# A chain of eight transformer layers on one core: three bias additions taken from TensorE to GpSimd and VectorE

## The reference

```python
x = x + _L0_attn_ref(_layernorm(x), ...)   # delta rule
x = x + _L0_ffn_ref(_layernorm(x), ...)    # the sine layer
x = x + _L1_attn_ref(_layernorm(x), ...)   # test-time MLP
x = x + _L1_ffn_ref(_layernorm(x), ...)    # dense experts
x = x + _L2_attn_ref(_layernorm(x), ...)   # softmax attention
x = x + _L2_ffn_ref(_layernorm(x), ...)    # channel mix
x = x + _L3_attn_ref(_layernorm(x), ...)   # blocked attention
x = x + _L3_ffn_ref(_layernorm(x), ...)    # routed experts
```

```python
# sine layer
hidden = jnp.einsum('bsd,df->bsf', x, W1) + b1
q = _quantum_transform(hidden, quantum_phases, quantum_weights_real, quantum_weights_imag)
return jnp.einsum('bsf,fd->bsd', jax.nn.relu(q), W2) + b2
# dense experts
gate_logits = jax.nn.softmax(x @ gate_w + gate_b, axis=-1)
# blocked attention, after the heads
return out @ out_w.T + out_b
```

## Time and profile before

| | us |
|---|---|
| median of 3 runs | 2658.85 |
| lowest, highest | 2652.12, 2659.35 |
| the profiled execution: its own time | 2652.55 |
| its span | 2650.7 |

### The profile page before, as it was taken

One profiled execution on the slowest core, in us unless ns is written; L12 is line 12 of the kernel. 1 busy time (PEld: TensorE's weight loads), 2 busy tenths in 40 slices (PEclk: granted clock), 3 DMA queues, 4 the chain that ended last, 5 costly groups with the idle time before them and its releaser, 6 DMA issues.

```text
span 2650.7 us, 63819 instructions
## 1 busy us (share of the span) xinstructions
PE 2092.7 (79%) x19997; PEld 1174.4 (44%) x20060; DVE 1837.0 (69%) x3796; ACT 1329.5 (50%) x2738; POOL 489.6 (18%) x920
## 2 busy tenths in 40 slices
PE   4449876788888778549999975569999999999755
PEld 2336543467777553224444434323333333333434
DVE  4856647556555447758888864579999999998371
ACT  4311105443333220327777763548888888888312
POOL 4312330034444210101111110001111111111103
PEclk9755558799999869869999997769999999999677
DMA  2342210000000000031111100221111111111001
GB/s 60 79 111 67 70 47 9 7 0 0 0 0 0 1 8 0 28 96 32 34 33 32 35 16 0 65 67 37 36 36 36 36 36 36 36 36 28 19 0 32
DMA packets 140453, 86.47 MB, mean 33 GB/s; under 512 B 67166, under 2 KB 119783, under 8 KB 140330
## 3 DMA queue, kind: packets, MB, share of 16 engines
q1 hardware_dynamic: 140330, 84.81, 12.8%
HBM read 56.88 MB, written 27.26 MB: 32 GB/s over the span
## 4 chain that ended last, share of the span: by engine, by line
PE 49%; DVE 28%; issue 10%; ACT 6%; DMA 2%; SPq 2%; POOL 2%; DVEq 1%; POOLq 0%; ACTq 0%; another core or an unknown queue 0%; PEldq 0%
PE psum L2098 9%; PE psum L2120 9%; DVE ba_blockmax L2330 8%; PE psum L2109 6%; DVE X L1285 2%; PE psum L2129 2%; PE psum L649 2%; PE psum L409 1%; ACT tt_sg L1638 1%; DVE dn_arena L929 1%; DVE tt_aT L1693 1%; PE psum L638 1%; PE psum L1600 1%; PE psum L672 1%; PE psum L1609 1%
## 5 line engine op out<-in xcount | busy, mean ns | idle before, releaser
L2330 DVE TENSOR_REDUCE ba_blockmax<-psum 128x16 f32<-128x1024 f32 x512 | 606.9, 1214 | 57.6 <-PE psum L2098 37.4
L2202 ACT ACTIVATE ba_pt<-psum 128x512 f32<-128x512 f32 x1024 | 554.0, 597 | 102.5 <-PE psum L2109 86.0
L2098 PE MATMUL psum<-ba_ks,ba_qs 64*128 64x512 bf16 x1024 | 343.7, 416 | 63.4 <-DMA ba_ks<-ba_kstk 21.2
L2332 DVE TENSOR_REDUCE sa_negmax<-psum 128x1 f32<-128x1024 f32 x256 | 304.4, 1221 | 85.8 <-PE psum L2098 77.9
L2202 ACT ACTIVATE sa_pt<-psum 128x512 f32<-128x512 f32 x512 | 269.9, 599 | 116.3 <-remote 58.7
L2120 PE MATMUL psum<-ba_pt,ba_vh 128*32 128x256 f32 x4096 | 314.1, 390 | 0.3
L2109 PE MATMUL psum<-ba_qs,ba_ks 64*128 64x512 bf16 x1024 | 313.7, 380 | 0.8 <-ACT ba_pt L2202 0.4
L2098 PE MATMUL psum<-sa_ks,sa_qs 96*128 96x512 bf16 x512 | 207.4, 410 | 30.8 <-DMA sa_ks<-sa_kstk 23.9
L2098 PEld LDWEIGHTS psum<-ba_ks,ba_qs 64*128 64x128 bf16 x1024 | 117.0, 148 | 253.8 <-issue 251.2
L2109 PE MATMUL psum<-sa_qs,sa_ks 128*128 128x512 bf16 x449 | 170.7, 383 | 1.8 <-ACT sa_pt L2202 1.6
L2120 PEld LDWEIGHTS psum<-ba_pt,ba_vh 128*32 128x32 f32 x4096 | 92.3, 108 | 154.8 <-issue 146.8
(11 more groups left out here) (479 smaller groups left out, 3902.6 us busy)
## 6 DMA issues: line engine op xcount, KB each, us to landing
ba_qs<-ba_qstk SPq DMA_DIRECT2D x128, 48.0 KB
ba_ks<-ba_kstk SPq DMA_DIRECT2D x128, 48.0 KB
dn_pst<-dn_arena SPq DMA_DIRECT2D x32, 128.0 KB, 2.4
dn_tst<-dn_arena SPq DMA_DIRECT2D x8, 512.0 KB, 5.8
dn_arena<-dn_tst SPq DMA_DIRECT2D x8, 512.0 KB, 4.4
dn_arena<-dn_pst SPq DMA_DIRECT2D x8, 512.0 KB, 5.9
ba_qs<-ba_qstk SPq DMA_DIRECT2D x128, 32.0 KB
ba_ks<-ba_kstk SPq DMA_DIRECT2D x128, 32.0 KB
```

What stands on the lines that cost most here:

```text
L2098: last = nc.tensor.matmul(bank(2 * slot + h), qs[b][0:KP, :].rearrange("p (a r) -> p r a", r=NTB)[:, r, :], ks[b][0:KP, h * HALF:(h + 1) * ...
L2202: nc.scalar.activation(pt[x_][:, :, h * P:(h + 1) * P].rearrange("p j (a m) -> p j a m", m=2), bank(4 + slot).rearrange("p (a j m) -> p j ...
L2330: ins = nc.vector.tensor_reduce(blockmax[g][:, r, :], src.rearrange("p (n s) -> p n s", s=BLOCK), AXX, ALU.max, negate=True)
L2332: ins = nc.vector.tensor_reduce(negmax[g][:, r:r + 1], src, AXX, ALU.max, negate=True)
```

## The change

The three one-row products are gone, and the first product of each group clears the bank in their place (start=True at n_ == 0 and f == 0, at n == 0, at m == 0). The biases are laid out as 128 equal rows, and are added

- in the sine layer and in the projection by GpSimd, directly to `k.X`, in eight instructions of 128x512 for each layer, issued back to back once the normalised tiles are all in `k.XT` and the weights are in. VectorE's own addition to the same tiles waits for a new semaphore `biased`, raised by one for each group;
- in the experts' gate by VectorE, whose copy out of PSUM becomes an addition.

```diff
@@ sine_ffn
-    b2 = k.sb("sf_b2", [1, GT], ctx=ctx)
+    b2 = k.sb("sf_b2", [P, D], ctx=ctx)
+    biased = k.sem("sf_biased")
 def add(i, g):
             v.wait_ge(outp[g], i + 2)
+            v.wait_ge(biased, i * 2 + g + 1)
+            k.plain(v)
-            nc.tensor.matmul(k.psum[:, 4 + g, :], k.ones_row[:, :], b2[:, :], start=True, stop=True)
             for n_ in range(GROUP):
                 for f in range(NF):
                     last = nc.tensor.matmul(k.psum[:, 4 + g, n_ * D:(n_ + 1) * D], act[g][:, f, n_ * P:(n_ + 1) * P],
-                                            w2[:, f, :], start=False, stop=True, skip_group_check=True)
+                                            w2[:, f, :], start=n_ == 0 and f == 0, stop=True, skip_group_check=True)
+    def gpsimd(p):
+        p.wait_ge(w_in, 64)
+        for g in range(2):
+            p.wait_ge(xt[g], NG // 2 + 1)
+        for n in range(NG):
+            xs = k.X[:, n * GROUP:(n + 1) * GROUP, :]
+            nc.gpsimd.tensor_tensor(xs, xs, b2[:, :].unsqueeze(1).to_broadcast([P, GROUP, D]), ALU.add).then_inc(biased, 1)
@@ dense_experts
-    gb = k.sb("de_gb", [1, GROUP * E], ctx=ctx)
+    gb = k.sb("de_gb", [P, E], ctx=ctx)
-                nc.tensor.matmul(bank, k.ones_row[:, :], gb[:, :], start=True, stop=True)
-                                            start=False, stop=True, skip_group_check=True)
+                                            start=n == 0, stop=True, skip_group_check=True)
-                nc.vector.tensor_copy(lg[:, bass.ds(i * 2 * GROUP + g * GROUP, GROUP), :],
-                                      k.psum[:, g, 0:GROUP * E].rearrange("p (n e) -> p n e", e=E)).then_inc(taken[g], 1)
+                nc.vector.tensor_tensor(lg[:, bass.ds(i * 2 * GROUP + g * GROUP, GROUP), :],
+                                        k.psum[:, g, 0:GROUP * E].rearrange("p (n e) -> p n e", e=E),
+                                        gb[:, :].unsqueeze(1).to_broadcast([P, GROUP, E]), ALU.add).then_inc(taken[g], 1)
@@ project_out
-                nc.tensor.matmul(k.psum[:, 2 + g, :], k.ones_row[:, :], ob[:, :], start=True, stop=True)
-                                            start=False, stop=True, skip_group_check=True)
+                                            start=m == 0, stop=True, skip_group_check=True)
                 v.wait_ge(outp[g], b + 1)
+                v.wait_ge(biased, 2 * b + g + 1)
+    def gpsimd(p):
+        p.wait_ge(w_in, 32)
+        for g in range(2):
+            p.wait_ge(xt[g], NG // 2 + 1)
+        for n in range(NG):
+            xs = k.X[:, n * GROUP:(n + 1) * GROUP, :]
+            nc.gpsimd.tensor_tensor(xs, xs, ob[:, :].unsqueeze(1).to_broadcast([P, GROUP, D]), ALU.add).then_inc(biased, 1)
```

More of the change, by code:

```diff
@@ L409, in second_product @@
                     last = nc.tensor.matmul(k.psum[:, 4 + g, n_ * D:(n_ + 1) * D], act[g][:, f, n_ * P:(n_ + 1) * P],
-                                            w2[:, f, :], start=False, stop=True, skip_group_check=True)
+                                            w2[:, f, :], start=n_ == 0 and f == 0, stop=True, skip_group_check=True)
             last.then_inc(outp[g], 1)
         one_ahead(t, NG, first_product, second_product)
-    k.add(sync=sync, vector=vector, scalar=scalar, tensor=tensor)
+    def gpsimd(p):
[5 more added lines that the diff above has]
+            nc.gpsimd.tensor_tensor(xs, xs, b2[:, :].unsqueeze(1).to_broadcast([P, GROUP, D]), ALU.add).then_inc(biased, 1)
+    k.add(sync=sync, vector=vector, scalar=scalar, tensor=tensor, gpsimd=gpsimd)
 def delta_net(k):
@@ L1244, in vector @@
         c = Chain(v, own)
+        v.wait_ge(w_in, 64)
         with v.Fori(0, NG // 2) as i:
@@ L2396, in attention, with project_out @@
     if blocked:
-        project_out(k, tag, O, H, HD, all_done, 1)
-def project_out(k, tag, O, H, HD, head_done, N):
+        project_out(k, tag, O, H, HD, all_done, 1, xt)
+def project_out(k, tag, O, H, HD, head_done, N, xt):
     nc, d, ctx = k.nc, k.dram, k.layer_ctx
@@ L2404, in project_out @@
     ow = k.sb(f"{tag}_ow", [P, D], ctx=ctx)
-    ob = k.sb(f"{tag}_ob", [1, GT], ctx=ctx)
+    ob = k.sb(f"{tag}_ob", [P, D], ctx=ctx)
+    biased = k.sem(f"{tag}_biased")
     oT = [k.sb(f"{tag}_ooT{z}", [P, S], ctx=ctx) for z in range(2)]
@@ L2859, in lay_out @@
                                                   col("L0_ffn_quantum_weights_real"), col("L0_ffn_quantum_weights_imag")], 1))
-    a["sf_b2"] = np.tile(a["L0_ffn_b2"], GROUP)[None]
+    a["sf_b2"] = np.tile(a["L0_ffn_b2"], (P, 1))
     a["dn_wqkv"] = np.concatenate([a[f"L0_attn_W{n}"] for n in "qkvb"], 1)
@@ L2871, in lay_out @@
     a["cm_mu"] = np.ascontiguousarray(np.stack([a["L2_ffn_mu_r"], a["L2_ffn_mu_k"]], 1))
-    a["de_gb"] = np.tile(a["L1_ffn_gate_b"], GROUP)[None]
+    a["de_gb"] = np.tile(a["L1_ffn_gate_b"], (P, 1))
     a["de_ew"] = np.ascontiguousarray(a["L1_ffn_expert_w"].transpose(1, 0, 2).reshape(D, -1))
@@ L2885, in lay_out @@
     a["ba_ow"] = np.ascontiguousarray(a["L3_attn_out_w"].T)
-    a["ba_ob"] = np.tile(a["L3_attn_out_b"], GROUP)[None]
+    a["ba_ob"] = np.tile(a["L3_attn_out_b"], (P, 1))
     for tag, heads in (("sa", 8), ("ba", 16)):
```

## The result

| | us |
|---|---|
| changed kernel, median of 4 runs | 2620.35 (2614.38 to 2622.89) |
| kernel before, median of 4 runs | 2659.1 (2652.12 to 2664.32) |
| ratio | 0.9853, interval 0.9824 to 0.9882 |
| span of the profiled executions, before and after | 2650.7, 2616.7 |

The account below looks back on a forecast made before the run. The prediction took TensorE's chain of waits, with the one-row products on it, as the bound in the three stretches. Its terms, −28.27 + 8.5 + 0.15 = −19.6 us, counted from 2655.7, gave 2636 us; range 2621 to 2651.

Parts of the forecast that it names:

- The products stand on the path, and go whole.: Sine layer, gate, projection: one-row products lie on TensorE's chain; removing them saves 11.55 + 4.47 + 12.25 = 28.27 us.
- Nothing late takes their place.: Sine layer, gate, projection: VectorE and ScalarE work uncovers no new wait; additions on VectorE's own path cost together 0.15 us.
- The GpSimd train holds the small columns, 8.5 us.: Sine layer's start: eight GpSimd additions hold eight of nine small VectorE steps, L309 to L320, delaying the first L366 8.5 us.
- The train before the projection ends just in time.: Before the projection: eight GpSimd additions end at 2463.0, ahead of L2352 at 2463.63; cover 0.6 us, cost put at 0.
- the heads' other work stays clear of it: Before the projection: the rest of VectorE's work for earlier heads reads PSUM or is early; no cost given.
- So the whole 28.3 us should go, if the clock keeps its pattern.: Sine layer, gate, projection: the full 28.3 us of removed products is gained, provided TensorE's clock pattern stays.
- Rival D: Sine layer stays at half clock, more idle and less work between waits: +26 to +35 us, 2667, slower; chance 0.06.
- Rival C: Sine layer and projection: gain partly lost to TensorE's clock, with a late train; together +8.7 us, 2645; chance 0.20.
- B: Sine layer's start: VectorE gets in between GpSimd's additions, 1.2 us lost in place of 8.5; −26.9, 2629; chance 0.20.
- The chance of 0.80 for faster: Whole kernel: chance 0.80 of being faster by over 0.3%, against 0.14 within 0.3% and 0.06 slower.

Follow-up runs that it names:

- e1: Changed kernel with an unused one-row product put back where the sine layer's and projection's bias products stood: 2662.03 us, ratio 1.0022 against the kernel before.
- e2: Changed kernel with an unused 128-row product put back where the sine layer's and projection's bias products stood: 2634.37 us, ratio 0.9915 against the kernel before.
- e7: Kernel before with its sine-layer and projection bias products kept but made 128 rows wide: 2632.77 us against 2662.58, ratio 0.9892.
- e8: Kernel before with only the projection's part of the change: 2636.06 us, ratio 0.9901 against the kernel before.

## Why the prediction was right and wrong

- **The products stand on the path, and go whole.** Right. L411 starts behind L378, and put back they cost their 1.1 us and more (e1, e2).
- **Nothing late takes their place.** Right: no new wait is seen in the chains of the three stages; ScalarE's copies hold 1.1 us of the projection's chain after as before, now 7.4% of it.
- **The GpSimd train holds the small columns, 8.5 us.** Right in mechanism, one VectorE step for each addition, tensor_scalar of four columns included. The size was 7.4 (27.4 - 19.9 us to the first L369) and 6.1 in the second profile (26.1 - 19.9): the additions follow each other 1.23 us apart, not 1.34, and the train began a step or two later in the columns. The 1.34 was from two additions of which the second needs the first. The Trainium skill's rule ("SBUF — State Buffer", Who interferes with whom) is borne out by these rows, also for tensor_scalar on four columns, which the forecast had left open.
- **The train before the projection ends just in time.** It did, and with more room than forecast: from 2436.17 it takes 9.90 us, to 2446.07, and the last head's step came at 2447.85. The cover was 1.8 us. But the forecast that the heads' other work stays clear of it was wrong: one step of the head before met the train and took 1.01 us, where its like took 0.22 in the kernel before. It isn't on the chain.

```profile
2442.67 1.01 DVE L2376 TENSOR_TENSOR XT<-ba_oS,ba_recip 128x64 f32<-128x64 f32 x1
```
- **"So the whole 28.3 us should go, if the clock keeps its pattern."** This is the step that failed: the sum gives the clock a term of 0, and no row is shown for that. The clock did not keep its pattern. Sine layer: -9.8 measured is -11.55 for the products, +7.4 for the train, +0.1, and -5.7 left over; the blocks of 32 passes alone went from 38.0 us (35.8% of 106) to 30.6 (eight of 3.83), and other pieces of the layer took 1.7 of these 7.4 back. Projection: -20.0 is -12.25 and -7.7. Gate and experts: -7.1 is -4.5 and -2.6. Together 16.0 us of the miss; e7 finds about 20 of clock in the first two when the products are kept. The other 3.2 of the 19.2 us are a train 1.1 us cheaper than forecast, less 2.9 that the untouched layers gave back, and 4.8 by which the medians lie further apart than the profiled executions; for the last two the record has no cause.
- **The gate's -2.6 can't be put down to the change.** Its loop, before and after, and two stretches of it after:

```profile
959.00:978.00 19.00, 18.91 (x80) 18.13 (x80) 1.34 (x7) 5.47 (x8) 0.00 (x0) 0.50 0.00 0
```
```profile
948.00:952.00 4.00, 2.81 (x24) 2.46 (x22) 0.38 (x2) 2.94 (x7) 0.00 (x0) 1.00 0.00 0
...
956.00:960.00 4.00, 4.00 (x20) 4.00 (x21) 0.57 (x3) 2.52 (x3) 0.00 (x0) 0.50 0.00 0
```

  Before, the loop ran at half clock from its start; after, it starts at full clock and falls to half, with no one-row product in it. But in e7 and e8, whose gate is that of the kernel before, it also starts at full clock and takes 16.9 and 17.2 us in place of 18.9, and in e2, whose gate is the changed one, it runs at 0.51 and takes 13.7 in place of 11.6.
- **Rival D** had the direction backwards. It reasoned that with the products gone each group has less work for the clock to see. The rows to doubt that stood there: TensorE was busy for 33.41 of 35 us in the projection, and its clock 0.60. An engine that is busy all the time at a low clock says that its busy time alone doesn't tell its clock. I read these two numbers side by side and drew only the price from them.
- **Rival C** priced the clock in the same wrong direction, and counted two turns in the projection where the chain has four (17.4% of 35 us is 6.1); **B** (a cheap train) did not occur.

The range failed by its lower end, as it held no case in which the clock improves by more than "a few us". The chance of 0.80 for faster was on the right side.

## What to carry to other kernels

A bias row added by a product of one row costs its own time (1.1 us at full clock, 2.0 at half, for 512 columns here) and may cost the clock of the products behind it; in the sine loop it did. Where TensorE is busy and its granted clock is low, ask how many rows its products use; try them wide, or take them off. And put GpSimd additions where VectorE's steps from SBUF to SBUF are not on the path: a train in front of a chain of tiny steps holds each step for a whole addition.

## What the runs showed of the hardware that was not expected

- In the sine loop a product's rows move the clock at equal instructions and columns: mean granted clock 0.84, 0.87, 0.96, 0.94 with 1, 32, 64, 128 rows; idle time in its place, 0.78. That it is the rows and not the power that the data draw isn't separated. The clocks with 32 and 64 rows and of idle time are of one profile each; one row stands at 0.82 to 0.84 in three (the kernel before and e8 among them), 128 rows at 0.94 in two (e7).
- A full row of busy time is no sign of a full clock: TensorE was busy for 33.41 of 35 us in the old projection at a granted clock of 0.60, and in the changed gate, with products of 128 rows and 8 columns alone, for 4.00 of 4.00 us at 0.50. The Trainium skill ("TensorE: Matmul & The Clock Gate", Part 1) ties the clock to how busy TensorE is; by these rows, "busy" in the profile is not what is meant.
- Behind a product of 128 rows the block is 0.2 us shorter than behind one of one row at the same clock (3.57 and 3.77 in the sine loop, 0.89 and 1.09 in the projection), and in the projection the product is as well (0.86 and 1.05). With 32 and 64 rows it is as with one: 3.77.
